# Cross-attention scores and maxima: one product of 128 output rows against four of 32

## The reference

```
q = (layernorm(x) @ Wq + bq)     # 512 latents, 16 heads of 32
k = (ctx @ Wk + bk)              # 8192 context rows, 16 heads of 32
v = (ctx @ Wv + bv)
scores = einsum('bhnd,bmhd->bhnm', q, k) / sqrt(32)
attn = softmax(scores, axis=-1)  # over the 8192 context rows
out = einsum('bhnm,bmhd->bnhd', attn, v)
```

## Time and profile before

| | |
|---|---|
| runs, median of 3 | 1570.58 us (1568.69 to 1570.84) |
| profiled execution | 1571.6 us |
| its span | 1569.6 us |
| mean granted TensorE clock | 0.950 |
| PE busy | 1434.4 us (91%) |
| DVE busy | 1144.6 us (73%) |
| ACT busy | 840.9 us (54%) |
| POOL busy | 841.9 us (54%) |
| PE's matrix instructions | 10760 |

### The profile page before, as it was taken

How to read it: one execution, slowest core, us unless ns; L and a number is a source line. 1 busy time by engine, 2 the same in 40 slices (tenths; PEclk the granted TensorE clock), 3 DMA queues, 4 the chain that set the end, 5 groups by cost and what they waited for, 6 DMA issues and landing times. The chain is left out here.

```text
span 1569.6 us, 31924 instructions
## 1 busy us (share of the span) xinstructions
PE 1434.4 (91%) x10760; PEld 616.4 (39%) x10760; DVE 1144.6 (73%) x1821; ACT 840.9 (54%) x1562; POOL 841.9 (54%) x322
## 2 busy tenths in 40 slices
PE   6999999969999999999999999999998587886998
PEld 3454444412333333333333333333333233454644
DVE  7477777769777776777767777867778764576596
ACT  4445444502666665656656666656667332475721
POOL 2122222241988886888879878968989701100011
PEclk9999999966999999999999999999999888898999
DMA  6577778770151212111111212111110041301400
GB/s 228 165 217 228 208 216 226 192 215 1 32 167 58 60 34 61 58 34 55 55 59 33 60 59 60 33 49 60 35 38 3 3 153 54 81 2 55 114 8 20
DMA packets 109853, 136.97 MB, mean 87 GB/s; under 512 B 22672, under 2 KB 90640, under 8 KB 107664
## 3 DMA queue, kind: packets, MB, share of 16 engines
q1 hardware_dynamic: 109712, 135.07, 29.8%
HBM read 86.01 MB, written 44.30 MB: 83 GB/s over the span
## 5 line engine op out<-in xcount | busy, mean ns | idle before, releaser
L1024 DVE TENSOR_REDUCE attend_part_max<-attend_pre_ps 128x1 f32<-128x512 f32 x1024 | 635.2, 682 | 181.6 <-PE attend_pre_ps L854 169.6
L1112 POOL TENSOR_TENSOR early<-early,attend_prob 128x1024 f32<-128x1024 f32 x224 | 660.4, 2948 | 72.8 <-ACT attend_prob L1002 56.4
L1002 ACT ACTIVATE attend_prob<-attend_s_ps 128x512 f32<-128x512 f32 x1024 | 531.1, 603 | 287.8 <-PE attend_s_ps L873 284.7
L854 PE MATMUL attend_pre_ps<-attend_k_stack,early 96*128 96x512 f16 x952 | 367.7, 386 | 13.3 <-issue 13.2
L873 PE MATMUL attend_s_ps<-early,attend_k_stack 97*128 (+1 forms) x1024 | 348.3, 383 | 15.7 <-ACT attend_prob L1002 15.7
L884 PE MATMUL attend_pv_ps<-attend_prob,attend_vh 128*32 128x512 f32 x2048 | 277.2, 614 | 0.0
L873 PEld LDWEIGHTS attend_s_ps<-early,attend_k_stack 97*128 97x128 f16 x1024 | 99.0, 98 | 168.7 <-ACT attend_prob L1002 104.3
L895 PEld LDWEIGHTS attend_den_ps<-attend_prob,ones 128*32 128x32 f32 x2944 | 92.9, 112 | 156.3 <-issue 156.2
L854 PEld LDWEIGHTS attend_pre_ps<-attend_k_stack,early 96*128 (+1 forms) x952 | 92.5, 97 | 126.5 <-issue 51.3
L895 PE MATMUL attend_den_ps<-attend_prob,ones 128*32 128x128 f32 x2944 | 129.8, 277 | 0.0
L1108 POOL TENSOR_TENSOR early<-attend_prob 128x1536 f32<-128x1536 f32 x16 | 56.5, 3529 | 115.4 <-ACT attend_prob L1002 113.6
(11 more groups left out here) (163 smaller groups left out, 1599.9 us busy)
## 6 DMA issues: line engine op xcount, KB each, us to landing
v_scratch<-project_v SPq DMA_DIRECT2D x16, 1024.0 KB, 5.7
attend_k_stack<-k_scratch SPq DMA_DIRECT2D x64, 256.0 KB, 3.5
attend_vh<-v_scratch SPq DMA_DIRECT2D x16, 1024.0 KB, 4.8
early<-in_ctx_dram SPq DMA_DIRECT2D x16, 768.0 KB, 7.2
k_scratch<-project_k_hi SPq DMA_DIRECT2D x64, 128.0 KB, 2.7
k_scratch<-project_k_lo SPq DMA_DIRECT2D x64, 128.0 KB, 2.9
attend_k_stack<-k_scratch SPq DMA_DIRECT2D x64, 128.0 KB, 3.5
late<-in_L_xattn_W_dram SPq DMA_DIRECT2D x2, 2048.0 KB, 11.2
```

The costliest lines, as they stand in the source:

```text
L854: nc.tensor.matmul(pre_ps[:, n % PRE_BANKS], q_stack[0:KROWS, h_of, j * P:(j + 1) * P], k_stack[0:KROWS, s_of, part * BLK:(part + 1) * BLK ...
L1002: nc.scalar.activation(prob[:, q % PSLOTS, t, :], s_ps[:, s_bank[BT * q + t]], ACT.Exp, scale=SCALE).then_inc(p_ready, 1)
L1024: nc.vector.tensor_reduce(part_max[:, s, j, part:part + 1], pre_ps[:, bank], AX.X, ALU.max).then_inc(pre_read, 1)
L1112: nc.gpsimd.tensor_tensor(sums, sums, prob[:, q % PSLOTS, 0:n], ALU.add).then_inc(pool_summed, 1)
```

## The change

Each product of 128 output rows in `pre`, `first_pre` and `scores` is written as four products of 32 output rows, with the same moving operand, each into its own 32 PSUM partitions; one semaphore increment stands on the last of the four. The operands in a loop pass no longer lie at an address computed from the head number: two new tiles, `q_pre` and `q_now`, hold the queries of one even and one odd head each, one pair for the maxima and one for the scores. SP copies them from `q_stack` by DMA, two at the start of each of the first two heads' loads and two in each head that loads, and TensorE waits for them (`q_pre_in`, `q_now_in`). ScalarE's `copy_row` writes the maximum into row 96 of `q_now`.

```diff
+            q_pre = sb("q_pre", [P, 2, T], F16)
+            q_now = sb("q_now", [P, 2, T], F16)
...
                 for s in range(2):
+                    sp.dma_start(q_pre[0:KROWS, s], q_stack[0:KROWS, s, :]).then_inc(q_pre_in[s], 16)
+                    sp.dma_start(q_now[0:KROWS, s], q_stack[0:KROWS, s, :]).then_inc(q_now_in[s], 16)
                     for c in range(CH):
                         load_keys(s, s, c)
...
                 def head(i, s, loads):
                     h = 2 * i + s
+                    if loads:
+
+                        sp.wait_ge(pre_ready, FIRST_TILES + TILES * (h - 1) + TT * (QUADS - AHEAD))
+                        sp.dma_start(q_pre[0:KROWS, s], q_stack[0:KROWS, h + 2, :]).then_inc(q_pre_in[s], 16)
...
                             load_keys(h + 2, s, c)
+                            if c == CH - 1:
+                                sp.dma_start(q_now[0:KROWS, s], q_stack[0:KROWS, h + 2, :]).then_inc(q_now_in[s], 16)
...
+                def pre_tile(bank, s, part, j):
+
+                    for c in range(P // HD):
+                        queries = slice(j * P + c * HD, j * P + (c + 1) * HD)
+                        last = nc.tensor.matmul(pre_ps[c * HD:(c + 1) * HD, bank, :], q_pre[0:KROWS, s, queries],
+                                                k_stack[0:KROWS, s, part * BLK:(part + 1) * BLK], start=True, stop=True)
+                    last.then_inc(pre_ready, 1)
...
                 def pre(i, s, q, j):
...
-                    h_of = h + 1 if q < QUADS - AHEAD else h + 2
                     n = turn_of[(q, j)]
+                    if (q, j) == (QUADS - AHEAD, 0):
+                        pe.wait_ge(q_pre_in[s], 16 * (i + 2))
...
-                    nc.tensor.matmul(pre_ps[:, n % PRE_BANKS], q_stack[0:KROWS, h_of, j * P:(j + 1) * P],
-                                     k_stack[0:KROWS, s_of, part * BLK:(part + 1) * BLK],
-                                     start=True, stop=True).then_inc(pre_ready, 1)
+                    pre_tile(n % PRE_BANKS, s_of, part, j)
...
                     if q == 0 and t == 0:
                         pe.wait_ge(row_set, h + 1)
+                        pe.wait_ge(q_now_in[s], 16 * (i + 1))
...
-                    last = nc.tensor.matmul(s_ps[:, s_bank[n]], k_stack[0:KROWS + 1, s, n * P:(n + 1) * P],
-                                            q_stack[0:KROWS + 1, h, :], start=True, stop=True)
+                    for c in range(P // HD):
+                        keys = slice(n * P + c * HD, n * P + (c + 1) * HD)
+                        last = nc.tensor.matmul(s_ps[c * HD:(c + 1) * HD, s_bank[n], :], k_stack[0:KROWS + 1, s, keys],
+                                                q_now[0:KROWS + 1, s, :], start=True, stop=True)
                     last.then_inc(s_ready, 1)
...
-                def copy_row(h, bank):
+                def copy_row(h, s, bank):
                     act.wait_ge(row_ready, h + 1)
-                    nc.scalar.activation(q_stack[KROWS:KROWS + 1, h, :], pre_ps[KROWS:KROWS + 1, bank, :],
+                    nc.scalar.activation(q_now[KROWS:KROWS + 1, s, :], pre_ps[KROWS:KROWS + 1, bank, :],
```

More of the change, by code:

```diff
@@ L710, in perceiver @@
             v_in = [sem(f"v_in{s}") for s in range(2)]
+            q_pre_in = [sem(f"q_pre_in{s}") for s in range(2)]
+            q_now_in = [sem(f"q_now_in{s}") for s in range(2)]
             pre_ready = sem("pre_ready")
@@ L830, in first_pre @@
                     n = FIRST_AT + k + (k >= FIRST_ROW)
+                    if k % TILES == 0:
+                        pe.wait_ge(q_pre_in[s], 16)
                     if k % (TILES // CH) == 0:
@@ L835, in first_pre @@
                         pe.wait_ge(row_set, 1)
-                    nc.tensor.matmul(pre_ps[:, n % PRE_BANKS], q_stack[0:KROWS, s, j * P:(j + 1) * P],
-                                     k_stack[0:KROWS, s, part * BLK:(part + 1) * BLK],
-                                     start=True, stop=True).then_inc(pre_ready, 1)
+                    pre_tile(n % PRE_BANKS, s, part, j)
                 def pre(i, s, q, j):
@@ L1006, in head @@
                         if q == ROW_AT and last >= 1:
-                            copy_row(h + 1, turn_of["row"] % PRE_BANKS)
-                copy_row(0, (FIRST_AT + FIRST_ROW) % PRE_BANKS)
+                            copy_row(h + 1, 1 - s, turn_of["row"] % PRE_BANKS)
+                copy_row(0, 0, (FIRST_AT + FIRST_ROW) % PRE_BANKS)
                 head(0, 0, True, 2)
```

## The result

Three runs of the changed kernel took 1519.67 us in the median (1517.62 to 1521.83), against 1570.58: a ratio of 0.9677, 95% interval 0.9657 to 0.9697, 50.9 us less. The profiled execution took 1521.83 with a span of 1519.8; the mean granted clock is 0.951. The forecast was 1532 in a range from 1513 to 1560.

The account below looks back on a forecast made before the run. TensorE was taken to bound the kernel, since VectorE and ScalarE wait for it. 1571.6 - 50.2 (holes) + 7.2 (wait) + 3.3 (other engines' quads) + 1.1 (SP) = 1533.0; the runs' median lies 1.0 lower, so 1532, range 1513 to 1560.

Parts of the forecast that it names:

- The two holes: TensorE idle 0.09 and 0.12 us per quad where output rows change between 128 and 32; both close, 50.2 us gained.
- The division at no cost: Four f16 products of 32 rows share the array fully, 0.22 us a round; cost nothing, rounding 19 us either way.
- The rival in which they don't share the array at full rate: Rounds of four f16 products take 0.26 instead of 0.22 us, giving 1605 us; chance 0.04.
- that of the lower clock: Narrow products no longer keep TensorE's higher clock: 310 us more, 1880 us; chance 0.02.
- The wait of score 3: Score 3 waits for score 0's exponential on ScalarE, 0.03 us later a quad: 7.2 us more, bounds 0 and 19.
- The quads that others pace: At q = 2 (VectorE) and q = 15 (ScalarE), 0.10 and 0.12 us a head are not gained: 3.3 us.
- SP: Two query copies ahead of the first keys start the stage 1.1 us later, bounds 0 and 2.0.
- The instruction stream: Rival: TensorE's stream limits at 68 ns per pair of weight load and product, giving 1650 us; chance 0.07.
- GpSimd: Rival: GpSimd becomes the bound, pairs of quads held at 6.18 us, gain halved to 1550 us; chance 0.08.

Follow-up runs that it names:

- run 1: The changed kernel with its query copies and waits but undivided products of 128 output rows: 1569.6 us, ratio 0.9976 to the kernel before.
- run 2: The changed kernel with each score and maximum product as two of 64 output rows instead of four of 32: 1589.7 us, ratio 1.0109.
- run 3: The changed kernel with only maximum tiles 0 and 3 of a quad divided in four, the other products of 128 output rows: 1566.1 us, ratio 0.9954.
- run 4: The changed kernel with only the maximum products divided in four, score products of 128 output rows: 1663.4 us, ratio 1.0565.
- run 5: The changed kernel with only the score products divided in four, maximum products of 128 output rows: 1723.2 us, ratio 1.0968.
- run 7: The changed kernel with score 3 placed behind pre 3 in each quad: 1514.8 us, ratio 0.9643.
- run 6: The changed kernel with the first query copies issued on SP behind the first keys (maxima) and the last keys (scores): 1519.1 us, ratio 0.9667.
- run 8: The changed kernel with GpSimd adding three tiles instead of two at q = 8 too: 1539.5 us, ratio 0.9780.
- run 9: The changed kernel, loop body untouched, with GpSimd adding three tiles at q = 8 in heads 0 and 1 alone: 1536.2 us, ratio 0.9785.
- run 10: The kernel of run 8 with 64 already met waits, packed into 32 instructions, ahead of the loop: 1520.5 us, ratio 0.9685.

## Why the prediction was right

**The two holes.** The step held in kind and size. Runs 1 to 5 show that a hole stands exactly where the width changes, and nowhere else. I had 0.21 us a quad. Over the steady quads the two distances have shrunk by 0.09 (0.309 to 0.220) and 0.12 (0.334 to 0.217), 0.206 together. A whole steady quad gained 0.225 (3.061 to 2.836), and 239 times that are 53.8 us; I had 50.2.

**What I missed in it.** The weighted sum became 0.022 us shorter, since its predecessor has its width (run 3): 5.3 us, which are in the 53.8. And ScalarE's copy into `q_now` gave 0.12 us at each q = 15 (run 1), 1.8 us. Both are favourable, and 7 us together.

**The division at no cost.** Right: rounds of four f16 products stand 0.22 apart, as undivided ones did. The rival in which they don't share the array at full rate is out, and with it that of the lower clock: 0.98 granted, as before.

**The wait of score 3.** This term was mis-sized: 0.03 us a quad, 7.2 in all. The seven distances of the eight rounds sum to 1.538 us where the undivided ones took 1.535, and giving ScalarE 0.22 us more (run 7) takes 0.016 from a steady quad. So it is between 0.7 and 3.8 us. Score 3 stands 1.09 behind score 0 as before; the exponential is just hidden.

**The quads that others pace.** I had 0.22 us a head, 0.10 at q = 2 and 0.12 at q = 15. Measured: q = 2 gained 0.12 in place of 0.225, and q = 15, against run 1, 0.13. That is 0.11 and 0.10 not gained.

**SP.** 1.1 us forecast, 1.24 measured from the stage's first issue. Run 6 shows that it is the order on SP: with the first keys ahead of the copy it is gone.

**The sum again**, with measured terms: -53.8 for the quads, +3.1 for q = 2 and q = 15 (15 x 0.205), -1.8 for the copy, +1.2 for SP, -51.3 us in all, against -50.9 between the medians. I had forecast 38.6, a quarter too little: what my 1532 lacked are the two small gains (7 us) and most of the wait (7.2, of which 0.7 to 3.8 came). Both errors go the same way, and the range held them because it was wide.

**The instruction stream.** 48 products pass in a quad of 2.83 us, 59 ns a pair, and no mean distance in the steady burst is longer than 0.23. The rival's price, from a stretch where the stream was not the limit, was wrong as a limit. The stream did show itself as a cost, but at the loop's jump, which no case of mine had (runs 8 to 10).

**GpSimd.** It came nearer than I said. Its timeline, from the third sum of a head to the first of the next:

```profile
1053.85 34.48 POOL L1134 TENSOR_TENSOR early<-early,attend_prob 128x1536 f32<-128x1536 f32 x11 [0.47 <-ACT attend_prob L1024]
...
1096.40 3.55 POOL L1130 TENSOR_TENSOR early<-attend_prob 128x1536 f32<-128x1536 f32 x1 [1.78 <-ACT attend_prob L1024]
```

The eleven sums are six of three tiles and five of two, in 34.48 us without a stop: 6.19 for a pair with its handoffs, where TensorE's two quads take 5.89. I had compared 5.83 with 6.00, so this comparison came out the wrong way round: within a head GpSimd is the slower, by 0.30 a pair. My other one, over the whole head, is what holds: 7 x 6.19 + 3.65 = 47.0 us of sums against 48.92. It lags by some 2 us, hardly anything waits for that with four `prob` slots (ScalarE twice, 0.5 us in all, from 400 to 1100 us), and it catches up where the missing sum would be, with 1.78 us idle. That the slots cover the lag I had not worked out; here luck helped. Run 10 gives it 1.1 us more a head, and its idle time there is down to 0.50.

## What to carry to other kernels

Where products of few output rows alternate with full ones on TensorE, count the changes of width and multiply by 0.1 us, as long as TensorE sets the pace: dividing the full ones into column groups costs nothing in the array's time here, and mixing widths within a burst is far worse than either pure form. In this kernel the rule is to divide all or none. And when a change makes a loop's body or what stands ahead of it longer or shorter, look at the idle time that ends in "issue" behind the jump before giving the difference to the change: 32 instructions ahead of the loop moved this kernel by 16 us.

## What the runs showed of the hardware

A change between 128 or 64 output rows and 32 costs 0.09 to 0.12 us in either direction; a change of contraction rows (96, 97, 128) or of type between neighbours of one width costs nothing that shows. Four f16 products of 32 rows with 512 columns run together in 0.22 us. Behind each jump back of these loops (2210 to 3746 TensorE instructions) TensorE pauses 2.2 to 3.1 us, and a second time for 1.2 to 2.2 us when the loop's top stands at position 86 of 256; with the low clock that follows, the passage is 3.1 us longer. That positions 30, 118, 197 and 198 are spared is what was seen; where exactly the border lies, and what a shorter loop would do, was not tried. Nor are 2 us of run 1's gain explained.
